# An MoE decoder layer in float32: an eight-place weight ring, one accumulator from expert 42 on, and routing flags scattered apart

## What is computed

```python
x = _layernorm(x + attention(x))      # 16 heads, decaying linear attention, gated
x = _layernorm(x + xattn(x))          # each token goes to 1 of 4 experts by its token id
# third block: 8 of 48 kept experts for each token
logits = x @ gate_weight.T                        # kept experts only
top_v, top_i = jax.lax.top_k(softmax(logits), 8)
top_v = top_v / jnp.sum(top_v, axis=-1, keepdims=True)
pos = jnp.sum(jnp.cumsum(oh, axis=0) * oh, axis=-1) - 1   # place in the expert, by token order
valid = pos < 192                                 # capacity
gu = jnp.einsum('ech,eoh->eco', xb, gate_up_proj)
g, u = jnp.split(gu, 2, axis=-1)                  # 192 each
out = jnp.einsum('eci,ehi->ech', silu(g) * u, down_proj)
final = jnp.zeros_like(x).at[tok].add(y * w[:, None])
x = _layernorm(x + final)
```

## Time and profile before

| What | us |
|---|---|
| Median of the three timed runs | 1000.11 (997.23 to 1002.01) |
| The profiled execution | 996.64 |
| Its span, first to last instruction | 994.8 |
| Stage B, 19 tiles | about 345 to 535 |
| From B to C | about 535 to 577 |
| Stage C, 48 experts | about 577 to 943 |
| Tail | about 943 to 994.8 |

### The profile page before, as it was taken

The page is one execution under the profiler, slowest core; times in us unless marked ns, Lnnn a source line. Parts: engine busy times, 40 slices in busy tenths (PEclk is TensorE's granted clock), DMA queues, the critical chain, the costliest instruction groups (busy, mean ns, idle before and its releaser), DMA issues.

```text
span 994.8 us, 17953 instructions
## 1 busy us (share of the span) xinstructions
PE 826.4 (83%) x5706; PEld 705.3 (71%) x5707; DVE 638.1 (64%) x1442; ACT 401.1 (40%) x805; POOL 453.5 (46%) x424
## 2 busy tenths in 40 slices
PE   6899999999997559988893189999999999999600
PEld 5778887877786348878882078888888888888500
DVE  6777567657765536777774747666676667675415
ACT  5332232333223213333221035665665665665404
POOL 0322432342343123444432047777677677776435
PEclk9999999999999679999996589999999999999855
DMA  9621211121111032222222169999999999999686
GB/s 321 241 97 44 68 61 42 42 84 42 42 62 34 11 122 70 84 99 97 89 77 78 23 178 258 276 277 259 268 278 254 281 273 259 274 273 269 112 268 240
DMA packets 79291, 154.92 MB, mean 156 GB/s; under 512 B 17136, under 2 KB 17264, under 8 KB 78864
## 3 DMA queue, kind: packets, MB, share of 16 engines
q1 hardware_dynamic: 57280, 99.42, 30.7%
q0 software_dynamic: 21968, 54.95, 22.8%
HBM read 110.25 MB, written 44.09 MB: 155 GB/s over the span
## 4 chain that ended last, share of the span: by engine, by line
PE 56%; DVE 17%; issue 10%; DMA 7%; POOL 6%; ACT 2%; DVEq 0%; POOLq 0%; SPq 0%; ACTq 0%
PE ps L879 17%; PE ps L583 14%; PE ps L892 10%; PE ps L868 3%; PE ps L689 2%; DVE arena L1268 2%; DMA w_lo<-y_rows 2%; POOL y_rows L1695 2%; DMA arena<-y_rows 2%; POOL arena L1671 1%; POOL x_rows L1693 1%; PE ps L611 1%; PE ps L620 1%; PE ps L724 1%; PE ps L629 1%
## 5 line engine op out<-in xcount | busy, mean ns | idle before, releaser
L879 PE MATMUL ps<-arena,raw 128*128 128x192 f32 x1152 | 198.8, 330 | 3.5 <-DVE arena L1548 3.1
L879 PEld LDWEIGHTS ps<-arena,raw 128*128 128x128 f32 x1152 | 189.8, 191 | 13.1 <-DVE arena L1548 8.6
L1737 POOL DMA_INDIRECT y_rows<-arena x96 | 153.4, 1598 | 92.6 <-issue 71.8
L1728 POOL DMA_INDIRECT w_lo<-x_rows,arena x96 | 103.5, 1078 | 55.1 <-issue 28.6
L583 PE MATMUL ps<-w_hi,x_hi 128*128 128x512 f32 (+1 forms) x332 | 78.2, 358 | 4.3 <-DVE x_lo L1310 3.5
L1577 DVE TENSOR_TENSOR w_hi<-raw,w_hi 128x512 fp32r<-128x512 f32 x48 | 33.2, 692 | 64.4 <-ACT w_hi L1081 53.9
L1064 ACT ACTIVATE arena<-ps,arena 96x512 f32<-96x512 f32 x48 | 32.8, 683 | 103.0 <-PE ps L892 103.0
L583 PE MATMUL ps<-w_lo,x_hi 128*128 128x512 f32 (+1 forms) x332 | 74.2, 346 | 0.0
L583 PE MATMUL ps<-w_hi,x_lo 128*128 128x512 f32 (+1 forms) x332 | 74.1, 346 | 0.0
L892 PE MATMUL ps<-w_hi,x_hi 128*96 128x512 f32 x192 | 63.4, 412 | 12.6 <-issue 6.0
L1624 POOL TENSOR_TENSOR arena<-arena,attn_pack 128x512 f32<-128x512 f32 x12 | 16.8, 1403 | 114.1 <-DVE arena L1203 114.1
(11 more groups left out here) (219 smaller groups left out, 1793.2 us busy)
## 6 DMA issues: line engine op xcount, KB each, us to landing
raw<-in_gu SPq DMA_DIRECT2D x48, 768.0 KB
raw<-in_dn SPq DMA_DIRECT2D x48, 256.0 KB
raw<-in_dn SPq DMA_DIRECT2D x48, 128.0 KB
y_rows<-zero SPq DMA_DIRECT2D x20, 256.0 KB
arena<-in_xT SPq DMA_DIRECT2D x16, 256.0 KB
x_res<-in_x SPq DMA_DIRECT2D x16, 256.0 KB, 2.8
raw<-in_ctxw SPq DMA_DIRECT2D x1, 4096.0 KB, 14.3
x_rows<-x1o SPq DMA_DIRECT2D x16, 256.0 KB, 2.0
```

The source lines that it names most:

```text
L879: m = pe.matmul(out, wgu[p][:, q, part * P:(part + 1) * P], xgT[:, p, q, :], start=(q == 0), stop=(q == KC - 1))
L1728: pool.indirect_dma_start(out=xg[:, place, h, :], out_offset=None, in_=x2_d, in_offset=bass.IndirectOffsetOnAxis(ap=place_token[:, n, h:h ...
L1737: pool.indirect_dma_start(out=(y_d, y2_d)[p], out_offset=bass.IndirectOffsetOnAxis(ap=place_token[:, n, h:h + 1].bitcast(U32), axis=0), in ...
```

## The change

1. **Weights.** Eight places for expert weights (RING). Places 0 to 3 fill raw, 4 to 6 a new tensor over the room of w_hi and w_lo, which are now freed after stage B, 7 lies in arena. SP issues experts 0 to 3 in stage B, 4 to 7 behind the load of the flags, and expert n + 8 when expert n's up product and split are done.
2. **Accumulators.** From expert 42 on (DUAL) every add goes to y_rows, and each waits for the landing of the one before. SP loads y2_rows into raw once expert 43's weights have been used and the odd adds up to 41 have landed.
3. **Flags.** Chosen or not is a tensor of its own, flag_rows, scattered by POOL right after the marking. The scatters of the weights and of the seed follow it, and the power of the tile stands ahead of all of them. Router products use two PSUM banks, and the route of tile 17 comes ahead of the normalising of tile 18.
4. **Places.** The running sum goes over 16 consecutive tokens of a partition, so the flags load with one run for each partition. The first group of eight experts is made in two halves. A further product (`spread_table`) brings the table into the layout of the indices in PSUM, without the way through DRAM. The seeds of the last two tiles are issued behind the gathers of experts 0 to 2; ACT and DVE wait for them before they write over x2o.
5. **Tail.** y_rows alone, seven pieces of two tiles and two of one, three at a time.

```diff
+RING = 8
+DUAL = 42
+PIECES = [(j, j + 2) for j in range(0, NT - 2, 2)] + [(NT - 2, NT - 1), (NT - 1, NT)]
...
+            def load_expert(n, slot):
+                sp.dma_start(wgu[slot], ...).then_inc(weights_in[slot], 16)
+                sp.dma_start(wdn[slot], ...).then_inc(weights_in[slot], 16)
+                sp.dma_start(wdn_rest[slot], ...).then_inc(weights_in[slot], 16)
...
+            for n in range(4):
+                load_expert(n, n)
...
+            sp.dma_start(whole(flag_rows), flags_d[0:TOK, :].rearrange("(p j) n -> p j n", j=NT)).then_inc(flags_in, 16)
+            sp.wait_ge(y1_made, SLOT_T)
+            sp.wait_ge(s_made, 2 * SLOT_T)
+            for n in range(4, RING):
+                load_expert(n, n)
+            with sp.Fori(0, E2 // RING - 1) as i:
+                for m in range(RING):
+                    sp.wait_ge(gu_made[m % 2], (RING // 2) * i + m // 2 + 1)
+                    sp.wait_ge(dn_split[m % 2], (RING // 2) * i + m // 2 + 1)
+                    load_expert(RING * i + m + RING, m)
...
+            for p in range(2):
+                sp.wait_ge(gu_made[p], (E2 - 4) // 2)
+                sp.wait_ge(dn_split[p], (E2 - 4) // 2)
+            sp.wait_ge(y_added[1], 32 * (DUAL // 2))
+            for q in range(4):
+                sp.dma_start(y2_all[:, 4 * q:4 * (q + 1), :], ...).then_inc(y2_in, 16)
...
             for p in range(2):
                 sp.wait_ge(y_added[p], 32 * (E2 // 2))
...
+                at_least(sp, y_in[q % 3], 16 * (q // 3))
+                sp.dma_start(y_all[:, slice(*PIECES[q]), :], rows_of(y_d, q)).then_inc(y_in[q % 3], 16)
...
-                at_least(pe, routed, 2 * k + p)
+                at_least(pe, routed, 2 * k + p - 1)
...
+            def spread_table(done, size=GE):
+                pe.wait_ge(tab_masked, done + 1)
+                pe.matmul(ps[0:HALF, 7, 0:size * NBB], spread[0:size * NA, :], tab[...], start=True, stop=True).then_inc(tab_spread, 1)
...
+            act.wait_ge(y_seeded[0], 16 * (SLOT_T - SLOT_T // 2))
+            act.wait_ge(y_seeded[1], 16 * (SLOT_T // 2))
             copy_x(0, 0)
...
             def b_tile(j, p, k, left, place):
                 if left == 2:
                     gather(j + 2, p, k + 1, (place + 2) % 4)
-                if is_later(j):
-                    scatter(j - 2, p, k - 1, (place - 2) % 4)
                 pool.wait_ge(mv_made, NT + 2 * k + p + 1)
...
                 pool.tensor_tensor(rstd2[:, :], ve2[:, :], minus_half[:, 0:1], ALU.pow).then_inc(rstd_made, 1)
+                if is_later(j):
+                    scatter_flags(j - 2, p, k - 1, (place - 2) % 4)
+                    if left:
+                        scatter_x2(j - 2, p, k - 1, (place - 2) % 4)
+                        seed_y(j - 2, p, k - 1, (place - 2) % 4)
...
             def c_scatter(n, p, k):
                 at_least(pool, y_added[p], 32 * k)
+                if n >= DUAL:
+                    pool.wait_ge(y_added[1 - p], 32 * (k + p))
...
+            for n in range(3):
+                c_gather(n)
+            for j in (SLOT_T - 2, SLOT_T - 1):
+                seed_y(*tile_of(j))
```

More of the change, by code:

```diff
@@ L312, in build @@
-        shift3 = sb("shift3", [P, NT])
+        raw_flat = raw[:, :, :, :].rearrange("p e k n -> p (e k n)")
+        y2_all = raw_flat.rearrange("p (j n) -> p j n", n=D)
+        with ExitStack() as until_c:
+            w_hi = until_c.enter_context(nc.sbuf_tensor("w_hi", [P, 4, KC, D], F32R))
+            w_lo = until_c.enter_context(nc.sbuf_tensor("w_lo", [P, 4, KC, D], F32R))
+        down_parts = sb("down_parts", [P, 2, 2, 2, D], F32R)
+        wdn_hi = [down_parts[:, 0, k] for k in range(2)]
@@ L830, in _ @@
             route((SLOT_T - 1) % 2, (SLOT_T - 1) // 2)
-            pe.wait_ge(tab_v, 2)
-            pe.wait_ge(c_half, 2)
-            for half in range(2):
-                js = slice(half * NT // 2, (half + 1) * NT // 2)
-                out = ps[:, half, 0:NT // 2 * E2]
-                pe.matmul(out, before_b[:, :], sel[:, js, :].rearrange("p j n -> p (j n)"), start=True, stop=False)
-                pe.matmul(out, ones_b[:, :], sel_so_far[:, :, js].rearrange("p n j -> p j n"),
-                          start=False, stop=True).then_inc(pos_made, 1)
@@ L856, in _ @@
-            pe.wait_ge(tstep, 11)
+                    table(g + 3)
+                if m == 7:
+                    spread_table(g + 3)
+            first, second = slice(0, GE), slice(GE, E2)
+            pe.wait_ge(c_half, 2)
+            ahead_of(first, 0, 1)
+            table(0, 0, GE // 2)
+            spread_table(0, GE // 2)
+            table(1, GE // 2, GE // 2)
+            spread_table(1, GE // 2)
+            ahead_of(second, 1, 2)
+            pe.wait_ge(tstep, 7)
             CT, CG, CY = 0, 2, 4
@@ L1350, in _ @@
             low_ctx(E1 - 1)
[L1353 removed]
+            BT, BS, BH, BY, BL = 0, 1, 3, 4, (7, 5)
             def hidden(p, k, half):
@@ L1476, in places @@
[L1476 to L1484 removed]
+            dve.tensor_scalar(ids_h[:, :], row_ids[:, :], -float(TOK), None, ALU.add).then_inc(c_half, 1)
```

464 lines of the change are left out of this document (240 added, 224 removed).

## The result

The changed kernel took 969.77 us (median of four runs, 968.94 to 970.97), the kernel before 999.97 us on the same chip (997.23 to 1002.01). The ratio is 0.9701, with a 95% interval of 0.9675 to 0.9726. The forecast was 973 us, with a range of 962 to 988. The profiled execution has a span of 969.1 us against 994.8, so 25.7 us less where 25.0 had been summed.

| Stretch | Before | After | Measured | Forecast |
|---|---|---|---|---|
| Start to second product of tile 3 | 390.56 | 392.96 | +2.4 | 0 |
| Fifteen tiles of stage B | 133.2 | 128.3 | -4.9 | -7.7 |
| Tile 18's second product to expert 0's product | 53.65 | 40.32 | -13.3 | -11.0 |
| Stage C, to TensorE's end | 365.9 | 361.3 | -4.6 | +2.0 |
| Tail, from there to the end | 51.5 | 46.2 | -5.3 | -8.3 |

The account below looks back on a forecast made before the run. Stage C was taken as TensorE's (busy 350.2 of 366 us), with gains possible in B, between B and C, and the tail. 7.7 + 11.0 - 2.0 + 8.3 = 25.0 less gave 971.6 or 975.1; middle 973 us, range 962 to 988.

Parts of the forecast that it names:

- Three places: Whole kernel: time can be gained in stage B, between B and C, and in the tail; the ring by itself gives none.
- Stage B, -7.7: Stage B: power ahead of the scatters takes fifteen tiles from 8.88 to 8.37 us each, 7.7 us less, bounds 0 to 12.8.
- The tile of 8.37: Stage B: time between second products of a tile without a scatter in its way, taken for all fifteen tiles.
- the rival with 991: Stage B: three scatters at 1.94 us keep POOL on the chain, 10.8 us more, 991 us; chance 0.03 (within 0.11).
- From B to C, -11.0: Between B and C: earlier flags and gathers, seeds landing last, expert 0's product at 566.4 against 577.43; 11.0 less, bounds 5 to 15.
- The burst of weights: Between B and C: 4.6 MB for experts 4 to 7 lies over the gathers; its rival: seeds land 6 later, 979 us, chance 0.13.
- Stage C, +2.0: Stage C: no gain from earlier weights, six small float32 products added on TensorE; 2.0 us more, bounds 0 to 3.
- The six products: Stage C: small float32 products, 96 x 128, on TensorE at 0.33 us each, 2.0 us more.
- so nothing: Stage C: weights land up to eight experts ahead, but TensorE did not wait for them before, hence no gain.
- Tail, -8.3: Tail: y2 loads early, adds from expert 42 go to y; end at 986.5, 8.3 us less, bounds 0 to 12.
- The last add's slip: Tail: adds waiting for each other slip 3.6 us, shrinking to 2 at expert 47; last add issued out at 950.0.
- six adds in file: Tail: each accumulating scatter lands 8.7 us after issue, six of them cost 30 us, 1001.6 us; chance 0.03.

Follow-up runs that it names:

- seeds_early: Changed kernel with the seeds of the last two slot tiles issued right behind the last two row scatters instead of behind six gathers; 969.51 us.
- before_pow: Kernel before with only POOL's power put ahead of the two scatters in each slot tile; 989.47 us, ratio 0.9908.
- weights_late: Changed kernel with the loads of experts 4 to 7 held until expert 0's rows have been gathered, seeds still behind the gathers; 973.51 us.
- rest_high: Changed kernel with the last 64 rows of the down weights of all eight places on partitions 64 to 127; 974.85 us.
- dual46: Changed kernel with the switch to one accumulator at expert 46 instead of 42; 970.20 us.
- both_junction: Changed kernel with last two tiles' seeds ahead of the gathers and loads of experts 4 to 7 held until expert 0's rows are there; 966.18 us.
- pow_behind: Changed kernel with POOL's power put back behind the scatters of two tiles ago, now three of them; 974.34 us.
- before_low: Kernel before with only the last 64 rows of each expert's down weights loaded to partitions 0 to 63 instead of 64 to 127; 988.30 us, ratio 0.9878.

## Why the prediction came out right, step by step

**Where it was to be gained.** Three places, none of them the ring itself: this held. TensorE waits for no weights in either kernel. What the ring did to the time came from the address of 64 rows, and from its burst of loads, which costs 3.1 us between B and C once the seeds no longer hide it (38.0 in seeds_early against 34.9).

**Stage B, -7.7: right mechanism, too large by 2.8.** The wait for the power went, as forecast, and what comes last next is TensorE's wait for o_hi on ACT, as forecast. The tile of 8.37 is real, since the power alone gives it (before_pow). The step that failed is "I take that tile's 8.37" for a kernel that also gets a third scatter, another order on DVE and a second router bank: something among these costs 0.18 a tile, no run shows which, and the term put nothing for it. POOL did not stay on the chain (the rival with 991): three scatters at 0.96 to 1.33 leave it idle 1.4 to 3.7 us before a tile's power.

**From B to C, -11.0: right to 2.3.** Counted from tile 18's second product: flags scatter at 12.4 forecast and 11.5 measured, flags in at 17.7 and 17.3, first gather at 27.8 and 27.0, gathers issued at 36.3 and 35.2, seeds landed at 41.9 and 39.6, product at 42.6 and 40.3. The seeds' landing is the term that was mis-sized: 3.0 was taken, 1.8 measured; of the rest 0.9 was there from the flags' scatter on. The copy of expert 0 is released by the seeds, not by a transpose. The burst of weights did not do what its rival feared: it held the gathers by 3.5 us, which the later seeds hid, and the seeds landed 1.8 us after their issue. The Trainium skill ("DMA: Bandwidth & Descriptors", section "Issuing engines are not separate DMA queues") says that the DMAs of all issuing engines share the same 16 DMA engines; weights_late agrees in both directions, with gathers 3.5 us faster and seeds 5.2 us slower than in the changed kernel.

**Stage C, +2.0: a small term about right, the large one missing.** The stage came out on the other side of nothing. The six products hold about 1.3 us, and 1.6 to 2.9 with all else in C. Missing was -6.2 (rest_high against the changed kernel), and "so nothing" is the sentence that failed: ACT and DVE, not TensorE alone, set the expert's length, and the diff changed what both read. The forecast took busy 350.2 of 366 for the bound and did not ask what the other 16 us were; 6.0 of them were the 25 waits before the down product.

**Tail, -8.3: too large by 3.0.** The last add's slip against the kernel before is 3.8 us, not 2: the two loaded landings took 7.8 and 5.9, not 5.5, and it hardly shrank, because issue, landing and start (3.15 + 3.4 + 0.3 = 6.85) are about as long as TensorE's expert there, 7.0; the forecast had let it shrink against 7.6, the mean of all 48. The first sum came 6.7 us after the last issue, where 7.2 was forecast. From DVE's first sum to ACT's end 24.9 us were forecast and 24.9 measured. The end after ACT is 6.0, not 4.3. Windows of the last us (DMA share and GB/s are the last two numbers):

```profile
962.00:964.00 2.00, 0.00 (x0) 0.00 (x0) 0.16 (x1) 1.03 (x2) 0.04 (x1) 0.50 1.03 385
964.00:966.00 2.00, 0.00 (x0) 0.00 (x0) 0.00 (x0) 0.00 (x0) 0.00 (x0) 0.50 0.33 127
966.00:968.00 2.00, 0.00 (x0) 0.00 (x0) 0.00 (x0) 0.00 (x0) 0.00 (x0) 0.50 0.00 0
```

The forecast let the whole time after ACT shrink with the last store. But over 3 us to the end at 969.1 move nothing, where about 3 us did in the kernel before (no traffic from 992 to 994.8), so this part did not shrink with the store.

**The start, 0: not shown to be the change.** One thing that differs between the two traces is the granted clock near the end of stage A. The window from 315 to 330 of the changed kernel (length, TensorE busy, granted clock, DMA share, GB/s):

```profile
315.00:330.00 15.00, 9.19 (x55) 0.50 0.13 37
```

Here it is 0.50, the level of 1.2 GHz throughout; in the kernel before it was 0.66. weights_late and dual46 have 0.50 as well and reach tile 3 at 392.95 and 392.94, the changed kernel at 392.96. But among the kernels with 0.66 to 0.68 the point lies anywhere from 390.56 (before) over 390.67 (both_junction) to 392.03 (before_pow, whose stage A is that of the kernel before) and 392.52 (pow_behind). So kernels with the same start differ by about 2 us, and these 2.4 us are put down to the execution; the clock in this window is a part of it at most. Of the four runs of the changed kernel the profiled one was the slowest.

**The sum** was right to 0.7 us by luck: 6.6 us of gain in stage C that it did not have and 2.3 more between B and C stood against 2.8, 3.0 and 2.4 us that were missing in B, in the tail and at the start. The range held the time, but the bounds of stage C's term (0 to 3 more) did not hold its -4.6. What was right is the three places, the chain between B and C step by step, and the wait that went in B. One rival was added up from another start: six adds in file puts its 30 us on 971.6, the others on 973; on 973 it is 1003, which changes no chance.

## What to carry to other kernels

An engine that is busy 96% of a stage may still not be its bound: look at its small repeated waits (25 of 0.24 us) and ask what ends them, for an address may be worth more than a ring of buffers (10.8 us here, and nothing in stage C from the ring). When a transfer is moved, look where it lands next: seeds alone gave 2.3 us, weights alone cost 4.9, both together gave 5.4. And try the smallest edit by itself: the power's place alone gave 7.7 us in stage B, and the 64 rows alone 10.8 in stage C of the kernel before.

## What the runs showed of the hardware that was not expected

Which partitions the instructions on ACT and DVE use decides whether they overlap. With 64 rows read from partitions 64 to 127, behind an instruction that begins at partition 0, the starts are 0.10 to 0.12 us further apart than with the rows read from 0 to 63 (0.71 against 0.61 us on DVE at 0.69 of duration), for the same work; three kernels show it in stage C's length. That it is the change of partitions between neighbours, and not the crossing inside one instruction, fits all rows shown, but no run was made to tell the two apart.

A gather on POOL that otherwise takes 0.91 to 1.75 us to issue took 4.63 beside DVE's one-hots in 16-bit numbers:

```profile
561.41 1.22 DVE L1529 TENSOR_TENSOR arena<-arena,ab_h 128x1024 f16<-128x1024 f16 x1
...
561.60 4.63 POOL L1790 DMA_INDIRECT xg<-x_rows,place_token  x1 [2.56 <-DMA y_rows<-arena,slot_token]
```

This gather took 3.92 to 4.63 in the changed kernel and in all its variants, each time beside these instructions, wherever they lay in time; in the kernel before the longest was 1.94, and in before_pow and before_low one took 2.5 beside such instructions. The Trainium skill ("SBUF — State Buffer", section "SBUF: two separate sides") names a port pair that DVE and GpSimd share. That this is the cause was not tried. What it costs was not measured either; it is the gather of expert 3, three experts ahead of its use.
